# Two layers of mixing and experts on one core: the softmax attention's loop over head pairs is written out, with both heads of a pair scored side by side

## The reference

```python
latent_kv = x @ w_kv_down                      # [2048,128] @ [128,128]
kv = latent_kv @ w_kv_up                       # [128, 2*1024]
k, v = kv[..., :HD], kv[..., HD:]              # 16 heads of 64
q = (x @ w_q).reshape(Bx, Tx, N_HEAD, HEAD_SIZE)
att = jnp.einsum('bqhd,bkhd->bhqk', q, k) * HEAD_SIZE ** -0.5
att = jnp.where(causal, att, -jnp.inf)
att = jax.nn.softmax(att, axis=-1)
y = jnp.einsum('bhqk,bkhd->bqhd', att, v).reshape(Bx, Tx, HD)
return y @ w_out
```

## Time and profile before

| | |
|---|---|
| median of 3 runs | 2755.13 us (2746.61 to 2756.91) |
| span of the profiled execution | 2757.3 us (no other time of that execution is given) |
| mean granted TensorE clock | 0.934 |
| TensorE, VectorE, ScalarE, GpSimd busy | 88%, 57%, 39%, 19% |
| the attention, first projection to output projection | 1634.5 to 2435.5 us of the span |
| the output projection | 2435.5 to 2467 us |

### The profile page before, as it was taken

How to read it: one execution, slowest core, us unless ns; L and a number is a source line. 1 busy time by engine, 2 the same in 40 slices (tenths; PEclk the granted TensorE clock), 3 DMA queues, 4 the chain that set the end, 5 groups by cost and what they waited for, 6 DMA issues and landing times. The chain is left out here.

```text
span 2757.3 us, 49484 instructions
## 1 busy us (share of the span) xinstructions
PE 2420.2 (88%) x18575; PEld 1810.4 (66%) x18575; DVE 1575.1 (57%) x3695; ACT 1082.8 (39%) x3096; POOL 523.8 (19%) x993
## 2 busy tenths in 40 slices
PE   4887998978989799898995879999999999978997
PEld 3776776767767677677774555556556556666765
DVE  6566675657656676566764755545545545533334
ACT  2544444434444344443442234434434434421112
POOL 5321333223322233223331000000000000000000
PEclk9999999999989899998997889989989989988999
DMA  3000000000000000000001000000000000010000
GB/s 130 1 2 1 1 1 2 1 1 1 1 1 1 1 1 1 2 1 2 1 1 55 0 0 1 1 2 1 1 2 1 1 2 1 1 62 1 1 0 15
DMA packets 5258, 20.96 MB, mean 8 GB/s; under 512 B 1848, under 2 KB 1984, under 8 KB 4032
## 3 DMA queue, kind: packets, MB, share of 16 engines
q1 hardware_dynamic: 5056, 17.95, 1.7%
HBM read 16.90 MB, written 1.05 MB: 7 GB/s over the span
## 5 line engine op out<-in xcount | busy, mean ns | idle before, releaser
L1443 DVE TENSOR_REDUCE b_nmax<-ps 128x1 f32<-128x1024 f32 (+7 forms) x256 | 194.0, 758 | 325.5 <-PE ps L1343 324.7
L817 DVE TENSOR_TENSOR prod<-ps,mt 128x128 f32<-128x128 f32 x512 | 147.2, 287 | 386.6 <-PE ps L687 257.5
L1339 PE MATMUL ps<-b_kT,b_qT 64*128 64x512 f32 (+3 forms) x768 | 328.1, 535 | 16.9 <-issue 15.4
L1410 ACT ACTIVATE b_prob<-ps,b_nmax 128x1024 f32<-128x1024 f32 (+7 forms) x256 | 189.6, 740 | 343.0 <-DVE b_nmax L1443 342.9
L322 PE MATMUL ps<-xT,taps 128*128 (+1 forms) x2176 | 303.7, 282 | 0.0
L322 PEld LDWEIGHTS ps<-xT,taps 128*128 128x128 f32 x2176 | 265.9, 191 | 11.6
L560 POOL COPY last<-di 128x512 f32<-128x512 f32 x130 | 81.1, 635 | 685.8 <-PE ps L548 484.2
L1339 PEld LDWEIGHTS ps<-b_kT,b_qT 64*128 64x128 f32 x768 | 127.4, 191 | 119.6 <-issue 102.8
L1072 PE MATMUL ps<-xTn,f_w 128*128 x352 | 168.4, 614 | 24.9 <-PEq L981 18.5
L1086 PEld LDWEIGHTS ps<-f_w,f_hT 128*128 128x128 f32 x1408 | 167.6, 193 | 31.6 <-issue 24.0
L1456 DVE COPY b_probT<-ps 128x512 f32<-128x512 f32 (+3 forms) x256 | 150.1, 586 | 63.1 <-PE ps L1365 61.3
(11 more groups left out here) (211 smaller groups left out, 4564.7 us busy)
## 6 DMA issues: line engine op xcount, KB each, us to landing
wtap<-in_taps SPq DMA_DIRECT2D x4, 1024.0 KB, 11.1
f_w<-in_f_w SPq DMA_DIRECT2D x2, 2048.0 KB
f_w<-in_f_w SPq DMA_DIRECT2D x2, 768.0 KB, 5.7
xT<-in_xT SPq DMA_DIRECT2D x2, 512.0 KB, 13.8
stream<-in_x_tok SPq DMA_DIRECT2D x1, 1024.0 KB, 12.0
wkv<-in_w_kv_up SPq DMA_DIRECT2D x1, 1024.0 KB, 8.4
out<-stream SPq DMA_DIRECT2D x4, 256.0 KB, 2.5
wraw<-in_WvT SPq DMA_DIRECT2D x1, 512.0 KB, 6.1
```

The lines of the kernel that those rows point to most:

```text
L817: ch.step(nc.vector.tensor_tensor(prod[:, b, :, :, :], zi, mtc[:, :, b, NB * c + i, :, :], ALU.mult))
L1339: mm = pe.matmul(bank[:, 0:c1 - c0], lhsT=qT[rows, f, b * T + i * P:b * T + (i + 1) * P], rhs=kT[rows, f, b * T + c0:b * T + c1], start=Tr ...
L1410: nc.scalar.activation(prob[:, u % 2, 0:n], src, ACT.Exp, bias=nmax[:, u % 4:u % 4 + 1], accum_out=total[:, w % 4, h:h + 1]).then_inc(sems ...
L1443: nc.vector.tensor_reduce(nmax[:, u % 4:u % 4 + 1], src, axis=AX.X, op=ALU.max, negate=True).then_inc(sems["max_done"], 1)
```

## The change

The loop over pairs becomes two groups of four pairs (`GP = 4`), written out. Each group has two blocks: one with its 48 projection pieces back to back, one with its 64 units.

- The projections run over all eight banks; ScalarE evicts the even pieces and VectorE the odd. A v piece covers one token tile of all four pairs. The weights are read from `wq` and `wkv` directly, and `pick`, `pair_w` and the two memsets go. q is kept in the place in `yT` that the unit's result later takes.
- The step is a whole unit w. Units of 8, 7, 6, 5 key tiles ("long") use banks 0 to 3 for scores, `prob[0]` and `probT[0]`; units of 1 to 4 ("short") banks 4 and 5, `prob[1]` and `probT[1]`. Scores are made in parts of 256 columns, head 0 and head 1 after each other, on different halves of the partitions and in different banks.
- The transposes of a unit, both heads' tiles and the spread reciprocal as the last, go in chunks of four through bank 6 alone; a chunk waits until the one before has been evicted. Between chunks stand score parts of w + 2 and value tiles of w − 1.
- Evictions of chunks: ScalarE takes chunks 0, 2 and 4 of long units, VectorE all others.
- The reciprocal is taken by VectorE with 128 columns out, the broadcast being in its input; GpSimd has no work left. The divide reads the turned reciprocal out of `probT`.
- `yT` is stored by sequence and time, and `project_out` makes two products of 64 output partitions for each step instead of one of 128.

```diff
-        with nc.Fori(0, NP // 2) as it:
+        units = [(m, b, i) for m in range(GP) for b in range(B) for i in order]
+        W = len(units)
+        def chunks(w):
+            return (2 * tiles(w) + 1 + 3) // 4
+        by_scalar = [not short(w) and c % 2 == 0 for w in range(W) for c in range(chunks(w))]
+        PIECES = [("q", m, s) for m in range(GP) for s in range(4)] + [("k", m, s) for m in range(GP) for s in range(4)]
+        PIECES += [("v", n, 0) for n in range(B * TT)]
+        for grp in range(NP // GP):
...
+            def scores_of(w, h):
+                if short(w):
+                    return ps[:, 4 + h, 0:tiles(w) * P]
+                return ps[:, 2 * h:2 * h + 2, :].rearrange("p k e -> p (k e)")[:, 0:tiles(w) * P]
...
+                    def scores(w, part):
+                        m, b, i = units[w]
+                        if part == 0 and w >= 2:
+                            pe.wait_ge(exp_done, 2 * (w - 2) + 2)
+                        c0, c1 = 256 * part, min(256 * part + 256, tiles(w) * P)
+                        last = c1 == tiles(w) * P
+                        for h in range(2):
+                            rows = slice(AD * h, AD * h + AD)
+                            mm = pe.matmul(scores_of(w, h)[:, c0:c1], lhsT=yT[rows, GP * grp + m, b * T + i * P:b * T + (i + 1) * P],
+                                           rhs=kT[rows, m, b * T + c0:b * T + c1], start=True, stop=not last,
+                                           skip_group_check=True)
...
+                    def turn(w, c):
+                        n, g = tiles(w), first_chunk[w] + c
+                        lo, hi = span_of(w, c)
+                        pe.wait_ge(exp_done, 2 * w + (1 if hi <= n else 2))
+                        if g >= 1:
+                            by_act, count = kept_by(g - 1)
+                            pe.wait_ge(t_kept_a if by_act else t_kept_v, count)
+                        for t in range(lo, hi):
+                            out = ps[:, 6, (t - lo) * P:(t - lo + 1) * P]
+                            if t < 2 * n:
+                                mm = pe.transpose(out, prob[short(w)][:, t // n, (t % n) * P:(t % n + 1) * P], cst["ident"][:, :])
+                            else:
+                                pe.wait_ge(recip_done, w + 1)
+                                mm = pe.transpose(out, inv[:, w % 2, :, :].rearrange("p h c -> p (h c)"), cst["ident"][:, :])
+                        mm.then_inc(t_done, 1)
...
+                        turns = chunks(w) if w < W else 1
+                        for c in range(turns):
+                            if w < W:
+                                turn(w, c)
+                            early = min(turns, 2 if short(w) else 3)
+                            if c < early:
+                                for part in range(ahead * c // early, ahead * (c + 1) // early):
+                                    scores(w + 2, part)
+                            late = turns - early + 1
+                            if c >= early - 1:
+                                for j in range(behind * (c - early + 1) // late, behind * (c - early + 2) // late):
+                                    values(w - 1, j)
...
+                    def row_max(w, h):
+                        dve.wait_ge(s_done, w + 1)
+                        k = (2 * w + h) % 8
+                        nc.vector.tensor_reduce(nmax[:, k:k + 1], scores_of(w, h), axis=AX.X, op=ALU.max, negate=True).then_inc(
+                            max_done, 1)
...
+                    for w in range(W + 1):
+                        if w < W:
+                            dve.wait_ge(exp_done, 2 * w + 2)
+                            nc.vector.reciprocal(inv[:, w % 2, :, :], total[:, w % 4, :].unsqueeze(2).to_broadcast([P, 2, AD])).then_inc(
+                                recip_done, 1)
+                        mine = [c for c in range(chunks(w)) if not by_scalar[first_chunk[w] + c]] if w < W else []
+                        for c in mine[:1]:
+                            keep_turned(w, c)
+                        if w + 2 < W:
+                            row_max(w + 2, 0)
+                        for c in mine[1:2]:
+                            keep_turned(w, c)
+                        if w + 2 < W:
+                            row_max(w + 2, 1)
+                        for c in mine[2:]:
+                            keep_turned(w, c)
+                        if w >= 1:
+                            divide(w - 1)
```

In `project_out`:

```diff
-                    mm = pe.matmul(ps[:, n // 4, (n % 4) * P:(n % 4 + 1) * P], lhsT=yT[:, m, n * P:(n + 1) * P],
-                                   rhs=wout[:, m, :], start=(m == 0), stop=(m == NP - 1), skip_group_check=True)
+                    for b in range(B):
+                        mm = pe.matmul(ps[b * TS:(b + 1) * TS, n // 4, (n % 4) * P:(n % 4 + 1) * P],
+                                       lhsT=yT[:, m, b * T + n * TS:b * T + (n + 1) * TS], rhs=wout[:, m, :], start=(m == 0),
+                                       stop=(m == NP - 1), skip_group_check=True)
```

More of the change, by code:

```diff
@@ L1192 @@
 TT = T // P
+GP = 4
 def softmax_attention(nc, ctx, cst, ps, weights, xT, yT):
+    HD = AH * AD
+    wdown, wq, wkv = weights
     with ExitStack() as own:
@@ L1206, in sem @@
             return ctx.enter_context(nc.semaphore("b_" + n))
-        HD = AH * AD
-        wdown, wq, wkv = weights
         latT = sb("latT", [P, B * T])
[L1211 to L1217, removed]
@@ L1218, in softmax_attention @@
-        recipT = sb("recipT", [P, 2, P])
-        x_row = xT[:, :].rearrange("c (n b t) -> c b n t", b=B, t=TS)
[L1220 to L1255, removed]
@@ L1258, in softmax_attention @@
[L1258 to L1291, removed]
@@ L1292, in softmax_attention @@
-        stage_end(nc, list(sems.values()))
-        order = [i for k in range(TT // 2) for i in (TT - 1 - k, k)]
[L1296 to L1308, removed]
@@ L1310, in softmax_attention @@
-        with nc.Fori(0, NP // 2) as it:
-            with nc.Block() as block:
[L1312 to L1322, removed]
+        kT = sb("kT", [P, GP, B * T])
@@ new lines, in softmax_attention, with tiles, short, kept_by @@
+        W = len(units)
+        def tiles(w):
+            return units[w][2] + 1
+        def short(w):
+            return w % 2
+        def chunks(w):
+            return (2 * tiles(w) + 1 + 3) // 4
+        first_chunk = [sum(chunks(x) for x in range(w)) for w in range(W + 1)]
+        by_scalar = [not short(w) and c % 2 == 0 for w in range(W) for c in range(chunks(w))]
+        def kept_by(g):
+            return by_scalar[g], sum(x == by_scalar[g] for x in by_scalar[:g + 1])
+        def through(w):
+            mine = by_scalar[:first_chunk[w + 1]]
+            return sum(mine), len(mine) - sum(mine)
@@ L1324, in _ @@
                 @block.tensor
                 def _(pe):
[L1326 to L1356, removed]
@@ L1358, in turn @@
-                    def turn(u):
-                        pe.wait_ge(sems["exp_done"], u + 1)
-                        if u >= 1:
-                            pe.wait_ge(sems["pt_kept_v"], u)
-                        for j in range(tiles(u)):
-                            if j == 4 and two_chunks[u] > 1:
-                                pe.wait_ge(sems["pt_kept_a"], two_chunks[u] - 1)
-                            mm = pe.transpose(ps[:, 4 + j // 4, (j % 4) * P:(j % 4 + 1) * P], prob[:, u % 2, j * P:(j + 1) * P],
-                                              cst["ident"][:, :])
-                            if j == min(4, tiles(u)) - 1 or j == tiles(u) - 1:
-                                mm.then_inc(sems["pt_done"], 1)
@@ L1388, in _ @@
-                    scores(0)
-                    for u in range(U + 1):
-                        if u + 1 < U:
-                            scores(u + 1)
-                        if u in at_step:
-                            piece(u)
-                        if u < U:
-                            turn(u)
-                        if u >= 2 and u % 2 == 0:
-                            values(u // 2 - 1)
+                    if grp == 0:
+                        for m in range(4):
+                            pe.matmul(ps[:, 4 + m, :], lhsT=wdown[:, :], rhs=x_row[:, m // 2, 8 * (m % 2):8 * (m % 2) + 8, :],
+                                      start=True, stop=True).then_inc(lat_done, 1)
@@ new lines, in _ @@
+                    for n, (kind, m, s) in enumerate(PIECES):
+                        bank = ps[:, n % 8, :]
+                        if n >= 8:
+                            by_act, count = kept_pieces(n - 8)
+                            pe.wait_ge(piece_kept_a if by_act else piece_kept_v, count)
+                        if grp == 0 and n == 4:
+                            pe.wait_ge(lat_kept, 4)
+                        if kind == "q":
+                            hp = GP * grp + m
```

(18 more changed lines are left out.)

201 lines of the change are left out of this document (111 added, 90 removed).

## The result

The changed kernel takes 2809.61 us (2806.74 to 2818.13), 1.022 times the kernel before [1.020, 1.025]: 2.2% slower. I had forecast 2810 and a chance of 0.68 for slower. Timed beside it, the kernel before took 2750.87 us, so the change costs 58.7 us where I had +55.

The account below looks back on a forecast made before the run. TensorE's issue was taken as the whole time. Attention 730, projections 82.6, latent 5.3, block edges 9, start clock 17, inner clock 15 make 859 against 801, +58; output projection −3.4 gives +55: 2810 us, range 2715 to 2885.

Parts of the forecast that it names:

- TensorE's issue bounded the kernel before: Second layer's attention: TensorE 99% busy in loop turns; summed prices gave 47.2 us per eight units, measured 46.7.
- The prices read from its timeline: TensorE's full-clock cost per step, such as scores 0.43 us per 256 columns, values 0.22 a tile, a projection tile 0.86.
- Row halves overlap: Scores: both heads' 256-column part takes 0.43 us; the rival of no overlap, 0.85 a part, +93 us, had chance 0.08.
- The doubtful size: Scores: a 128-column part of both heads taken as 0.32 us, between 0.21 by columns and 0.43 by weight loads.
- What TensorE gains it waits away: Attention, per eight units: 35.2 us of work and 10.4 idle, 45.6 in all, against 41.8 before.
- the walk: Step-by-step timing of the engines' queues through eight attention units, n = 8,1,7,2,6,3,5,4 key tiles: 45.6 us.
- The rival in which VectorE's queue holds less than walked: Transposes wait less for their one bank: under 7.0 us idle per eight units; 2727 at half, 2643 without; chance 0.20.
- The sign that VectorE would be busy for over 60%: VectorE's share of the attention window was to rise from 52% to over 60% if the forecast was right.
- The wide reciprocal: VectorE's 128x128 reciprocal takes 1.10 us, 8.8 per eight units; rival of 0.29 us as a copy, 2757, chance 0.07.
- The clock inside the blocks: Attention: 35 us of 730 at half clock, costing 15 us; the rival of a third, costing 104, 2899, had chance 0.10.
- each block's start: Low clock as a block begins: 6.6 us for each attention block, 4 for the second projection block, 17 in all.
- The output projection: 128 pairs of 64-column tiles at 0.22 us make 28.2 for 31.6 before, a gain of 3.4 us.

Follow-up runs that it names:

- 4: The changed kernel with all score parts of head 0 before those of head 1, so row halves do not alternate: 3014.3 us, 1.098 of the kernel before.
- 1: The changed kernel with VectorE's reciprocal narrow again (2 columns) and GpSimd spreading it to 128: 2758.2 us, 1.004 of the kernel before.
- 2: The changed kernel with ScalarE also evicting chunks 0 and 2 of short units: 2762.8 us, 1.007 of the kernel before.
- 3: The changed kernel with the edits of 1 and 2 together: 2743.2 us, 0.999 of the kernel before.
- 6: On top of 3, VectorE divides before the second maximum in long units: 2727.0 us, 0.993 of the kernel before.
- 5: The changed kernel with thirty useless bf16 products after chunk 0 of each 4-tile unit: 2786.3 us, 1.015 of the kernel before.
- 7: On top of 6, ScalarE evicts every chunk but the second of a unit: 2709.6 us, 0.987 of the kernel before.
- 8: On top of 7, VectorE takes the next short unit's reciprocal before the second maximum in long units: 2687.0 us, 0.977 of the kernel before.

## Why the prediction was right, point by point

- **TensorE's issue bounded the kernel before.** The prices read from its timeline held: a part of both heads 0.64 with its fixed 0.21, projections 40.8 us for 48 tiles (41.3), the output projection 28.2 (28.2). The sum of 96.7 for the projections before should read 98.4 (96 x 0.90 + 12); nothing is worked out from it.
- **Row halves overlap.** Shown by 4. The doubtful size also settled: a 128-column part of both heads takes 0.43 with its fixed 0.21, so 0.22, near the lower of its bounds, where I took 0.32. The rows of the changed kernel:

```profile
1957.08 0.49 PE L1334 MATMUL ps<-b_kT,b_yT 64*128 64x128 f32 x4
1957.51 0.28 PE L1339 MATMUL ps<-above_diag,ident 128*128 128x128 bf16 x2
```

- **What TensorE gains it waits away.** Shown: eight units without low clock take 44.7 us, the walk gave 45.6. Of it the profile counts 8.9 us as idle, for about 10 forecast. The profile counts the last 0.17 us of a record before a wait as busy and the walk as idle, so the two splits agree better than they look. The rival in which VectorE's queue holds less than walked needed under 7.0 us and fell. The sign that VectorE would be busy for over 60% did not come: 58%, for the reciprocal was cheaper than I took it and low clock stretched the window.
- **The wide reciprocal.** The direction was right and the size 17% high: 943 ns for 1.10 us, and for the 1.2 us estimated beside it. At the five places where it stands in the way this would make 0.8 us of the 0.9 us by which the walk was long; all together 16 x 0.9 = 14 us too much. The walk's parts were not compared one by one, so that the rest of it is exact is not shown. Its cost to the kernel is shown by 1: 51 us, some 17 of it by the clock.
- **The clock inside the blocks.** Mis-sized the other way. I put 35 us of the blocks at half clock, and 6.6 us of loss for each block's start, 28 us in all. The two blocks stood at 0.93 and 0.92: 2 x (0.07 x 383.6 + 0.08 x 386.3) = 115 us at half clock, with 0.45 us lost for each about 52. That is 24 us more than forecast. It is read from the longest of the four executions, 8.5 us above their median and with a mean granted clock of 0.924 where the others had 0.927 to 0.931, so in the median it is less. Against it stand the 14 us of the walk and the 4 us of low clock that I gave the second projection block, which stood at 1.00:

```profile
2072.00:2113.50 41.50, 40.67 (x95) 17.67 (x93) 16.61 (x24) 14.16 (x24) 0.00 (x0) 1.00 0.00 0
```

- **The output projection.** The price was right and the reason for the gain was not. I set 28.2 at full clock against 31.6 that hold 5.6 us at half clock; at full clock the stage before would take 28.7. So some 2.9 of the 3.4 us are clock, and that the changed stage stood at 1.00 is luck: the prediction had no term for it.
- **Adding it up.** The attention with its projections and edges runs from 1638.4 to 2501.3, 862.9 us, for a forecast of 859 and 801 before: +62. The output projection gives 3.4 back. The change does not touch the other stages: those ahead ended 3.9 us later in this execution (1638.4 for 1634.5), and those behind took 3.6 us less (2529.5 to 2816.2 for 2467 to 2757.3). Together that is the 59 us between the two spans.

For the fixes, my expectations failed where a wait was one engine further back than I looked, in runs 2, 3 and 6, and in run 4, which had no term for the clock.

## What to carry to other kernels

Half the array's time saved on a bound engine is worth nothing if its results then stand in another engine's queue: walk one period of the new order on every engine, with each instruction's place in its queue, before counting the gain. When an engine looks free by its total (VectorE 58%), look at what stands directly in front of the instruction that others wait for; here making one instruction narrow again (with its spread on GpSimd), moving two small ones and giving copies to an idle engine turned 2.2% slower into 2.3% faster. Moving an instruction forward also delays what it passes, as run 6 shows. Where a wait falls on another engine's buffer reuse, follow it one engine further before calling the edit done.

## What the runs showed of the hardware

- A reciprocal of 128 columns takes 943 ns on VectorE where one of 2 takes 155: 6.3 ns a column, about six times that of a copy (0.29 us for 128 columns, 0.69 for 512: 1.04 ns a column). The wide one reads its two values through a broadcast; no run has one of 128 columns without it, but 16 columns without it (253 ns) give 7.0 ns a column. The row of the changed kernel:

```profile
L1456 DVE RECIPROCAL b_inv<-b_total 128x128 f32<-128x128 f32 x128 | 120.7, 943 | 1.9 <-ACT b_prob_long L1401 1.8
```

- Low clock came with pauses of 1 to 3 us in a TensorE that was busy four fifths of the time, and cost 0.39 to 0.46 us for each microsecond (runs 4 and 5). With the pauses shorter (runs 7 and 8) most stretches of eight units stood at 1.00.
- I had not expected run 4: TensorE is busier there (51.4 of 57.8 us, against 37.4 of 46.3), its longest pause is shorter (2.2 us of idle time for 2.75), and the clock is lower, 0.78 to 0.88. What differs is that single row halves of the array work one at a time. No run here separates that from the rest, so its cause stays open.
